# Order of VectorE's work in the adapter layer: experts chosen ahead of the turning of the next tile

## The chip, the cores and the metric

One Trainium2 chip, one of its cores. The time is the device time of one execution in microseconds (us); smaller is better.

## What is computed

64 sequences of 64 channels by 512 features go through two layers: a conditioned spline FFN, then an adapted linear layer (LoRA adapter chosen per sequence) whose output goes through a mixture of eight experts, two per token. The change is in the stage that computes the adapted layer and the routing of the second layer:

```python
H = jnp.einsum('btd,od->bto', x, W)
xa = jnp.einsum('btd,brd->btr', x, A[adapter_idx])
delta = jnp.einsum('btr,bor->bto', xa, Bm[adapter_idx]) * scalings[adapter_idx][:, None, None]
z = (H + delta).reshape(-1, 512)
top_w, sel = jax.lax.top_k(z @ gate_w.T, 2)
tw = jnp.zeros((n, 8)).at[arange(n)[:, None], sel].add(softmax(top_w))
out = einsum('end,ne->nd', down(silu(gate(z)) * up(z)), tw)
x = x + out
```

## The kernel before

The program has four stages: preparing the weights (about the first 60 us), the first FFN, the adapted layer (`adapted_layer`, about 500 to 660 us of the profiled execution), and the experts.

`adapted_layer` goes over 4096 tokens in 8 tiles of 512 (t = 0 to 7), each cut into four sub-tiles of 128 tokens (s = 0 to 3). Tiles 0, 1, 6 and 7 are written out, 2 to 5 are a loop with two tiles per pass. Each engine has a queue of its own, in the order in which the code is written, and all orders meet at semaphores. No scheduler moves anything.

Per tile t:

- TensorE (PE) multiplies x1 by the adapters' A for the whole tile (12 matmuls, L1439 to L1441, bank XA). Then come eight products of 15 matmuls (L1428), `product(t, b, s, half, chunks)`: the output row of 520 columns (512 outputs and 8 logits) is cut into two halves, the right half (half 1, which has the logits) of s = 0 to 3 first, then the left half (half 0) of s = 0 to 3. The first two right halves run their first 12 matmuls while VectorE and ScalarE scale and split `xa`, and then their last three. A product may start when its PSUM bank has been copied out: s = 0 and 2 share a bank in each half, as do s = 1 and 3. Last come the two small matmuls of `ranks(t)` (L1413, L1414), which count for each token the rows that its experts have before it. They wait for `both_ready`. In tile 6 (`is_late`) PE leaves after two left halves, and the rest of it and its ranks stand in tile 7.
- ScalarE (ACT) rounds `xa` (L1489), rounds the next tile's x1 in four pieces (`high`, L1475, waits for `x1_loaded`), copies each product out of PSUM (`copy`, L1484), rounds two pieces of the early experts' weights (L1505, waits for `early_loaded`), and takes the exponential of the logits' gap (`shares`, L1479). Its order in tiles 2 to 5: xa, high 0 and 1, copy of right halves 0 and 1, early pieces, high 2, right half 2, high 3, right half 3, the left halves, with the exponential after the third of them.
- VectorE (DVE) scales xa (L1617), makes its remainder (L1621), and for each s makes the remainder of the next tile's x1 (`low`, L1542) and turns that x1 into token order (`turn`, L1548), with the early weights' remainders (L1632) at s = 1. Then it chooses the two experts (`choose`, L1563 to L1583, a chain of small instructions that ends with `both_ready`), and makes the shares and row numbers (`enter`, L1596 to L1609). `choose` waits for the copies of the right halves 2 and 3.
- SyncE (SP) issues DMAs. `next_x1(t + 2)` loads x1 of the tile after the next (L403, two DMAs). There is one x1 buffer, so it waits until tile t + 1 has been remaindered and turned (`x1t_low`, `tok_turned`). Behind it stand `store_out(t + 1)` (L1364, four DMAs of the turned x1) and `load_early(t + 1)` (L363, two DMAs of early weights).
- GpSimd (POOL) waits for the row numbers and then scatters the tile's rows with eight indirect DMAs (L1403), each pair behind a small instruction (L1401).

Of the kernel before, what the change touches and what calls it, by code (L numbers as in the profile page):

```python
# [29 lines left out]
LSUB = LTILE // P  # L30
# [1241 lines left out]
def adapted_layer(nc, alloc, sem, psum, ident, small, idle, lower, ones, tok_ids, out_tiles, x1, x1_loaded, load_x1,  # L1272
# [5 lines left out]
    with ExitStack() as scope:  # L1278
# [52 lines left out]
        def is_late(t):  # L1331

            return isinstance(t, int) and t == LNT - 2

        def is_last(t):
            return isinstance(t, int) and t == LNT - 1

        def xa_of(t):
            return (xa_high[1], xa_low[1]) if is_last(t) else (xa_high[0], xa_low[0])
# [17 lines left out]
        with nc.Block() as block:  # L1357
# [50 lines left out]
            @block.tensor  # L1408
            def _(pe):
                def ranks(t):  # L1410

                    pe.wait_ge(both_ready, t + 1)
                    nc.tensor.matmul(psum[RANKS][:, 0:LSUB * NE], lower[:, :], both[:, :, :].rearrange("p s e -> p (s e)"), start=True, stop=False)  # L1413
                    nc.tensor.matmul(psum[RANKS][:, 0:LSUB * NE], ones[:, :], chosen[:, 0:LSUB, :].rearrange("p s e -> p (s e)"),  # L1414
                                     start=False, stop=True).then_inc(filled[RANKS], 1)

                def product(t, b, s, half, chunks):

                    hi, lo = x1t_hi[b], x1t_lo[b]
                    xa_hi, xa_lo = xa_of(t)  # L1420
                    bank, rows = Z[s % 2][half], slice(s * P, (s + 1) * P)
                    if 0 in chunks:
                        pe.wait_ge(drained[bank], use(t, s) + 1)
                    for k in chunks:
                        x_high, x_low = (hi[:, k, rows], lo[:, k, rows]) if k < DK else (xa_hi[:, rows], xa_lo[:, rows])
                        for i, (x, w) in enumerate(((x_high, w_hi), (x_high, w_lo), (x_low, w_hi))):
                            last = k == DK and i == 2
                            ins = nc.tensor.matmul(psum[bank][:, 0:HALFW], x, w[:, k, half * HALFW:(half + 1) * HALFW],  # L1428
                                                   start=(k == 0 and i == 0), stop=last)
                    if DK in chunks:  # L1430
                        ins.then_inc(filled[bank], 1)

                def body(t, n, b, has_next, first):

                    pe.wait_ge(x1t_low, LSUB * (t + 1))
                    hi, lo = x1t_hi[b], x1t_lo[b]
                    pe.wait_ge(drained[XA], t + 1)
                    for k in range(DK):
                        nc.tensor.matmul(psum[XA][:, :], a_hi[:, k, :], hi[:, k, :], start=(k == 0), stop=False)  # L1439
                        nc.tensor.matmul(psum[XA][:, :], a_hi[:, k, :], lo[:, k, :], start=False, stop=False)  # L1440
                        ins = nc.tensor.matmul(psum[XA][:, :], a_lo[:, k, :], hi[:, k, :], start=False, stop=(k == DK - 1))  # L1441
                    ins.then_inc(filled[XA], 1)
                    if is_last(t):
                        ranks(t - 1)

                    for s in range(2):
                        product(t, b, s, 1, range(DK))

                    pe.wait_ge(xa_done, t + 1)
                    for s in range(2):  # L1450
                        product(t, b, s, 1, [DK])
                    for s in range(2, LSUB):
                        product(t, b, s, 1, range(DK + 1))
                    if is_late(t):
                        for s in range(EARLIER):
                            product(t, b, s, 0, range(DK + 1))
                        return
                    if is_last(t):
                        for s in range(EARLIER, LSUB):
                            product(t - 1, 1 - b, s, 0, range(DK + 1))  # L1460
                        ranks(t)
                        nc.tensor.matmul(psum[XA][:, 0:NE], ones[:, :], chosen[:, LSUB, :], start=True, stop=True).then_inc(counted, 1)
                    for s in range(LSUB):
                        product(t, b, s, 0, range(DK + 1))
                    if not is_last(t):
                        ranks(t)

                steps(pe, body)

            @block.scalar  # L1470
            def _(act):
                def high(t, b, s):
                    if s == 0:
                        act.wait_ge(x1_loaded, 32 * (t + 1))
                    nc.scalar.activation(x1t_hi[b][:, :, s * P:(s + 1) * P], x1[:, :, s * P:(s + 1) * P], ACT.Copy).then_inc(x1t_high, 1)  # L1475

                def shares(t):
                    act.wait_ge(gap_ready, t + 1)
                    nc.scalar.activation(expo[:, :], gap[:, :], ACT.Exp).then_inc(expo_ready, 1)  # L1479

                def copy(t, b, s, half):
                    bank = Z[s % 2][half]
                    act.wait_ge(filled[bank], use(t, s) + 1)
                    nc.scalar.activation(z_out[b][:, s, half * HALFW:(half + 1) * HALFW], psum[bank][:, 0:HALFW], ACT.Copy).then_inc(drained[bank], 1)  # L1484

                def body(t, n, b, has_next, first):

                    act.wait_ge(drained[XA], t + 2)
                    nc.scalar.activation(xa_of(t)[0][:, :], xa[:, :], ACT.Copy).then_inc(xa_split, 1)  # L1489
                    if first and b == 0:  # L1490
                        copy(t, b, 0, 1)
                        copy(t, b, 1, 1)
                    if has_next:
                        for s in range(2):
                            high(t + 1, 1 - b, s)
                    if not first:

                        act.wait_ge(rows_stored[b], 16 * 2 * LSUB * n)
                    if not (first and b == 0):
                        copy(t, b, 0, 1)  # L1500
                        copy(t, b, 1, 1)
                    act.wait_ge(early_loaded, 16 * EARLY * (t + 1))
                    for e in range(EARLY):
                        to, _, raw = early_piece(t, b, e)
                        nc.scalar.activation(to, raw, ACT.Copy).then_inc(early_high, 1)  # L1505
                    for s in range(2, LSUB):
                        if has_next:
                            high(t + 1, 1 - b, s)
                        copy(t, b, s, 1)
                    if is_late(t):  # L1510
                        for s in range(EARLIER):
                            copy(t, b, s, 0)
                        shares(t)
                        return
                    if is_last(t):
                        for s in range(EARLIER, LSUB):
                            copy(t - 1, 1 - b, s, 0)
                        shares(t)
                    for s in range(LSUB):
                        copy(t, b, s, 0)  # L1520
                        if s == LSUB - 2 and not is_last(t):
                            shares(t)

                for s in range(LSUB):
                    high(0, 0, s)
                steps(act, body)

                nc.scalar.activation(idle[:, 63:64], small[:, 0:1], ACT.Silu)
                act.wait_ge(ctl_ready, 1)
                fetch_quads(act, 0, 0, (2, 3), rows_there)  # L1530

            @block.vector
            def _(dve):
# [78 lines left out]
                def body(t, n, b, has_next, first):  # L1612
# [11 lines left out]
                    for s in range(LSUB):  # L1624
                        if has_next:
                            low(t + 1, 1 - b, s)
                            turn(t + 1, s)
                        if s == 1:
                            for e in range(EARLY):
                                hi, lo, raw = early_piece(t, b, e)  # L1630
                                dve.wait_ge(early_high, EARLY * t + e + 1)
                                ins = nc.vector.tensor_tensor(lo, raw, hi.bitcast(F32), ALU.subtract)  # L1632
                                ins.then_inc(*((early_low, 1) if has_next else (weights_loaded, LOADS)))
                    choose(t, b)
                    if not is_late(t):
                        enter(t, n, b, first)

# [376 lines left out]
```

## Time and profile before

| | us |
|---|---|
| median of 3 runs | 1139.07 |
| lowest, highest run | 1135.13, 4557.15 |
| the profiled execution's own time | 1139.03 |
| span of its profile | 1137.3 |
| PE busy in the span | 1047.3 (92%) |
| DVE, ACT, POOL busy | 693.9, 473.1, 655.5 |

The span is the time between the first and the last instruction of the profile; the 1.7 us around it are launch and end. Tiles of the adapted layer follow each other every 18.4 to 18.8 us in the middle.

### The profile page before, as it was taken

Reading aid. Unit: us, or ns where it says so; the run is one execution under the profiler, and the core shown is the slowest. Engines: PE = TensorE matmul, PEld = TensorE weight load, DVE = VectorE, ACT = ScalarE, POOL = GpSimd, SP = SyncE. Lnnn points to the kernel's source line nnn. Section 1 sums busy time; section 2 is a strip of 40 time slices with the busy share of each in tenths; the row PEclk is TensorE's granted clock in tenths of the full one; section 3 lists DMA queues with packets and bytes.
Section 4 is the critical chain, followed back from the end, with each engine's and each line's share of the span. In section 5 each row is a group of like instructions: output and inputs, shape, how many; then the busy total and the mean of one; then the engine's idle time right before and its main releaser. Section 6 shows DMA issues by size and latency. Waiting matters only on the chain. (4 is left out here: it accounts for less than half of the span.)

```text
span 1137.3 us, 35583 instructions
## 1 busy us (share of the span) xinstructions
PE 1047.3 (92%) x12060; PEld 969.1 (85%) x12061; DVE 693.9 (61%) x1478; ACT 473.1 (42%) x964; POOL 655.5 (58%) x889
## 2 busy tenths in 40 slices
PE   1679999999999999879999949999999999999995
PEld 1669999999999999779999938999999999999994
DVE  8945666666776666447676735555555555555553
ACT  4245776777767767524333212222222222222221
POOL 6568999999999999603455533333333333333333
PEclk9868999999999999969999969999999999999998
DMA  6052555455555553446878658586767676745453
GB/s 263 1 165 102 199 177 183 164 197 200 184 174 200 175 183 128 184 131 199 275 236 278 193 177 234 97 230 145 182 146 174 144 179 142 186 83 83 84 87 61
DMA packets 126612, 188.32 MB, mean 166 GB/s; under 512 B 26040, under 2 KB 89656, under 8 KB 123104
## 3 DMA queue, kind: packets, MB, share of 16 engines
q1 hardware_dynamic: 58560, 130.96, 34.4%
q0 software_dynamic: 16432, 36.78, 16.4%
q10 hardware_dynamic: 51584, 20.12, 7.1%
q8 instruction: 21, 0.34, 0.1%
q14 instruction: 15, 0.12, 0.0%
HBM read 108.37 MB, written 81.83 MB: 167 GB/s over the span
## 5 line engine op out<-in xcount | busy, mean ns | idle before, releaser
L1760 POOL TENSOR_TENSOR idle<-small 128x1 f32<-128x1 f32 x212 | 71.1, 338 | 269.9 <-DMA out<-result,scatter_at 194.7
L1803 PE MATMUL banks<-slots,zt_hi 128*128 x568 | 189.3, 333 | 16.1 <-DVE zt_lo L1914 16.1
L1805 PE MATMUL banks<-slots,zt_lo 128*128 x568 | 183.9, 324 | 0.0
L1804 PE MATMUL banks<-slots,zt_hi 128*128 x568 | 183.9, 324 | 0.0
L985 POOL TENSOR_TENSOR in_lo<-inner,in_hi 128x512 fp32r<-128x512 f32 x128 | 164.4, 1291 | 31.9 <-ACT in_hi L1133 31.6
L1222 DVE TENSOR_TENSOR inner<-silu,banks 128x512 f32<-128x512 f32 x128 | 87.9, 687 | 113.7 <-ACT silu L1128 109.5
L1871 ACT ACTIVATE ht_hi<-banks 128x384 fp32r<-128x384 f32 x71 | 35.0, 492 | 253.5 <-PE banks L1813 246.0
L1776 POOL DMA_INDIRECT out<-result,scatter_at x71 | 111.6, 1572 | 28.1 <-issue 26.2
L1803 PEld LDWEIGHTS banks<-slots,zt_hi 128*128 128x128 f32 x568 | 107.5, 189 | 16.3 <-issue 16.3
L979 POOL TENSOR_TENSOR f_lo<-f_sum,f_hi 128x256 fp32r<-128x256 f32 x128 | 110.7, 884 | 3.1 <-ACT f_hi L1124 3.1
L1128 ACT ACTIVATE silu<-banks 128x512 f32<-128x512 f32 x128 | 76.3, 596 | 77.1 <-PE banks L1054 75.9
L1804 PEld LDWEIGHTS banks<-slots,zt_hi 128*128 128x128 f32 x568 | 107.6, 189 | 0.0
L1805 PEld LDWEIGHTS banks<-slots,zt_lo 128*128 128x128 f32 x568 | 107.4, 189 | 0.0
L1133 ACT ACTIVATE in_hi<-inner 128x512 fp32r<-128x512 f32 x128 | 80.5, 629 | 42.3 <-DVE inner L1222 31.0
L1944 DVE TENSOR_TENSOR result<-banks,share 128x512 f32<-128x512 f32 x71 | 49.1, 692 | 76.9 <-DMA out<-result,scatter_at 55.6
L1054 PE MATMUL banks<-f_hi,gu_hi 64*128 64x256 f32 x512 | 87.1, 335 | 7.3 <-DVE inner L1222 4.4
L1881 ACT ACTIVATE zt_hi<-banks 128x512 fp32r<-128x512 f32 x72 | 43.1, 598 | 104.7 <-DVE banks L384 91.3
L1212 DVE TENSOR_REDUCE f_sum<-banks 128x256 f32<-128x512 f32 x128 | 82.1, 683 | 5.8 <-PE banks L1040 5.4
L1823 PE MATMUL banks<-slots,ht_hi 128*128 x213 | 84.2, 395 | 1.3 <-DVE ht_lo L1918 1.3
L1825 PE MATMUL banks<-slots,ht_lo 128*128 x213 | 84.4, 396 | 0.0
L1070 PE MATMUL banks<-in_hi,down_hi 32*128 32x256 f32 x1024 | 83.7, 316 | 0.6 <-POOL in_lo L985 0.6
L1824 PE MATMUL banks<-slots,ht_hi 128*128 x213 | 84.0, 394 | 0.0
(255 smaller groups left out, 3136.7 us busy)
## 6 DMA issues: line engine op xcount, KB each, us to landing
late_dram<-split_part SPq DMA_DIRECT2D x32, 816.0 KB, 5.2
slots<-late_dram SPq DMA_DIRECT2D x24, 1088.0 KB, 5.6
x<-rows_dram ACTq DMA_DIRECT2D x278, 64.0 KB, 3.2
raw_part<-in_late_w SPq DMA_DIRECT2D x16, 816.0 KB
x_t<-in_x_t SPq DMA_DIRECT2D x16, 512.0 KB
x_both<-in_x_tok SPq DMA_DIRECT2D x16, 512.0 KB
x_both<-in_x_res SPq DMA_DIRECT2D x16, 512.0 KB, 3.4
x1t_dram<-x_both SPq DMA_DIRECT2D x16, 512.0 KB, 6.3
```

Of the source, the lines that this page charges most:

```text
L979: nc.gpsimd.tensor_tensor(f_lo[:, g, :], f_sum[g % F_SUMS][:, :], f_hi[:, g, :].bitcast(F32), ALU.subtract).then_inc(f_done, 1)
L985: nc.gpsimd.tensor_tensor(in_lo[:, cs, :], inner[u % 2][:, :, :], in_hi[:, cs, :].bitcast(F32), ALU.subtract).then_inc(in_done, 1)
L1054: ins = nc.tensor.matmul(gu_bank[:, h, m * TILE:(m + 1) * TILE], w[rows, m, cols], f[rows, u, :], start=(i == 0), stop=(i == 2))
L1070: ins = nc.tensor.matmul(out_bank[r][:, cols], w[rows, c, :], x[rows, c, :], start=(c == 0 and i == 0), stop=(c == IC - 1 and i in (2, 4)) ...
L1222: nc.vector.tensor_tensor(inner[u % 2][:, :, :], silu[u % 2][:, :, :], gu_bank[:, :, TILE:2 * TILE], ALU.mult).then_inc(gu_drained, 1)
L1776: nc.gpsimd.indirect_dma_start(out, bass.IndirectOffsetOnAxis(ap=scatter_at[b][:, 0:1], axis=0), result[b][:, :], None, compute_op=ALU.add ...
L1803: nc.tensor.matmul(psum[bank][:, 0:FD], zt_hi[b][:, k, :], w_high, start=(k == 0), stop=False)
L1804: nc.tensor.matmul(psum[bank][:, 0:FD], zt_hi[b][:, k, :], w_low, start=False, stop=False)
L1805: ins = nc.tensor.matmul(psum[bank][:, 0:FD], zt_lo[b][:, k, :], w_high, start=False, stop=(k == DK - 1))
L1823: nc.tensor.matmul(psum[OUT[b]][:, :], ht_hi[:, f, :], w_high, start=(f == 0), stop=False)
L1824: nc.tensor.matmul(psum[OUT[b]][:, :], ht_hi[:, f, :], w_low, start=False, stop=False)
L1825: ins = nc.tensor.matmul(psum[OUT[b]][:, :], ht_lo[:, f, :], w_high, start=False, stop=(f == FC - 1))
```

## The change

Three calls move and nothing is added or left out. VectorE makes the four turns of the next tile's x1 between `choose` and `enter` instead of one behind each `low`. ScalarE takes the exponential after the second copy of a left half instead of the third. TensorE makes `ranks(t)` ahead of the last left half instead of behind it.

```diff
@@ PE
                     for s in range(LSUB):
                         product(t, b, s, 0, range(DK + 1))
-                    if not is_last(t):
-                        ranks(t)
+                        if s == LSUB - 2 and not is_last(t):
+                            ranks(t)
@@ ACT
                     for s in range(LSUB):
                         copy(t, b, s, 0)
-                        if s == LSUB - 2 and not is_last(t):
+                        if s == 1 and not is_last(t):
                             shares(t)
@@ DVE
                     for s in range(LSUB):
                         if has_next:
                             low(t + 1, 1 - b, s)
-                            turn(t + 1, s)
                         if s == 1:
...
                     choose(t, b)
+                    if has_next:
+                        for s in range(LSUB):
+                            turn(t + 1, s)
                     if not is_late(t):
                         enter(t, n, b, first)
```

VectorE in tile 0, between the remainder of xa and the choice (L1542 is `low`, L1548 `turn`, L1632 and its new number L1631 the early weights), the difference:

```order
-L1542 TENSOR_TENSOR x1t_lo<-x,x1t_hi 128x4x128
-L1548 STREAM_TRANSPOSE x_tok<-x 128x4x4x32
-L1542 TENSOR_TENSOR x1t_lo<-x,x1t_hi 128x4x128
-L1548 STREAM_TRANSPOSE x_tok<-x 128x4x4x32
-L1632 TENSOR_TENSOR slots<-slots 128x544 x2
-L1542 TENSOR_TENSOR x1t_lo<-x,x1t_hi 128x4x128
-L1548 STREAM_TRANSPOSE x_tok<-x 128x4x4x32
-L1542 TENSOR_TENSOR x1t_lo<-x,x1t_hi 128x4x128
-L1548 STREAM_TRANSPOSE x_tok<-x 128x4x4x32
+L1542 TENSOR_TENSOR x1t_lo<-x,x1t_hi 128x4x128 x2
+L1631 TENSOR_TENSOR slots<-slots 128x544 x2
+L1542 TENSOR_TENSOR x1t_lo<-x,x1t_hi 128x4x128 x2
```

The four transposes have gone from here.

VectorE in the same tile, from the end of `choose` (L1583) to the start of `enter` (L1596), the difference:

```order
 L1581 TENSOR_TENSOR staging<-staging 128x32
 L1583 TENSOR_TENSOR chosen<-chosen,staging 128x8 x4
+L1548 STREAM_TRANSPOSE x_tok<-x 128x4x4x32 x4
 L1596 TENSOR_SCALAR total<-expo 128x4
 L1597 RECIPROCAL staging<-total 128x4
```

They stand here now, behind the 16 steps of the choice; the next x1 load, the stores of the turned x1 and the early weights' load wait for the last of them on SP's queue.

TensorE at the end of tile 0 before (L1413 and L1414 are the ranks, L1439 and L1440 belong to the next tile):

```order
L1428 MATMUL banks<-w_lo,xa_hi 128x260
L1428 MATMUL banks<-w_hi,xa_lo 128x260
L1413 MATMUL banks<-staging,lower 128x32
L1414 MATMUL banks<-chosen,ones 128x32
L1439 MATMUL banks<-x1t_hi,a_hi 128x512
L1440 MATMUL banks<-x1t_lo,a_hi 128x512
```

And at the end of the third left half now:

```order
L1428 MATMUL banks<-w_lo,xa_hi 128x260
L1428 MATMUL banks<-w_hi,xa_lo 128x260
L1413 MATMUL banks<-staging,lower 128x32
L1414 MATMUL banks<-chosen,ones 128x32
L1428 MATMUL banks<-w_hi,x1t_hi 128x260
L1428 MATMUL banks<-w_lo,x1t_hi 128x260
```

The ranks stand 15 matmuls sooner, ahead of the product of the last sub-tile.

## Rows read from the trace of the kernel before

**Rows 1.** Windows: length, busy of PE, PEld, DVE, ACT, POOL; clock, DMA share, GB/s

```profile
502.00:508.20 6.20, 5.46 (x13) 4.30 (x14) 3.09 (x6) 0.00 (x0) 0.00 (x0) 0.50 0.24 69
...
564.90:583.70 18.80, 17.88 (x138) 17.16 (x137) 12.31 (x42) 6.89 (x16) 10.14 (x12) 1.00 0.80 263
```

**Rows 2.** Timeline of PE: start, length, instruction, idle before it and what ended it

```profile
502.74 0.80 PE L1439 MATMUL banks<-x1t_hi,a_hi 128*128 128x512 f32 x1 [4.26 <-DVE x1t_lo L1542]
...
524.17 0.41 PE L1413 MATMUL banks<-staging,lower 128*128 128x32 f32 x2 [0.97 <-DVEq L1584]
...
580.15 0.31 PE L1413 MATMUL banks<-staging,lower 128*128 128x32 f32 x2
...
580.52 0.48 PE L1439 MATMUL banks<-x1t_hi,a_hi 128*128 128x512 f32 x1
...
588.05 0.39 PE L1428 MATMUL banks<-w_hi,x1t_hi 128*128 128x260 f32 x1 [0.92 <-ACT staging L1484]
```

**Rows 3.** Timeline of DVE: tile 0's turns, then tiles 1, 3, 6 and 7

```profile
502.60 2.49 DVE L1548 STREAM_TRANSPOSE x_tok<-x 128x512 f32<-128x512 f32 x4
...
519.87 0.70 DVE L1548 STREAM_TRANSPOSE x_tok<-x 128x512 f32<-128x512 f32 x1
...
537.82 0.14 DVE L1563 TENSOR_REDUCE top<-x_both 128x4 f32<-128x32 f32 x1
...
573.29 0.70 DVE L1548 STREAM_TRANSPOSE x_tok<-x 128x512 f32<-128x512 f32 x1
574.05 0.19 DVE L1563 TENSOR_REDUCE top<-x_both 128x4 f32<-128x32 f32 x1
...
576.89 0.77 DVE L1583 TENSOR_TENSOR chosen<-chosen,staging 128x8 f32<-128x8 f32 x4
...
583.69 0.69 DVE L1617 TENSOR_TENSOR xa<-banks,adapter_scale 128x512 f32<-128x512 f32 x1 [1.93 <-issue]
...
629.71 0.14 DVE L1563 TENSOR_REDUCE top<-staging 128x4 f32<-128x32 f32 x1
...
643.61 0.19 DVE L1563 TENSOR_REDUCE top<-x_both 128x4 f32<-128x32 f32 x1 [0.76 <-issue]
```

**Rows 4.** Timeline of ACT in tiles 0, 1, 3 to 4, and 7

```profile
515.27 0.62 ACT L1475 ACTIVATE x1t_hi<-x 128x512 fp32r<-128x512 f32 x1
...
533.42 1.21 ACT L1505 ACTIVATE slots<-slots 128x544 fp32r<-128x544 f32 x2 [1.05 <-DMA slots<-in_early_w]
...
535.32 0.62 ACT L1475 ACTIVATE x1t_hi<-x 128x512 fp32r<-128x512 f32 x1
...
573.56 0.39 ACT L1484 ACTIVATE x_both<-banks 128x260 f32<-128x260 f32 x1 [1.30 <-PE banks L1428]
...
584.95 1.14 ACT L1475 ACTIVATE x1t_hi<-x 128x512 fp32r<-128x512 f32 x2
...
588.16 1.21 ACT L1505 ACTIVATE slots<-slots 128x544 f32 x2
...
640.73 1.21 ACT L1505 ACTIVATE slots<-slots 128x544 fp32r<-128x544 f32 x2 [1.25 <-DMA slots<-in_early_w]
```

**Rows 5.** SP's DMA issues behind the turns of tile 3

```profile
574.24 1.32 SPq L403 DMA_DIRECT2D x<-x1t_dram  x2
575.75 4.74 SPq L1364 DMA_DIRECT2D out<-x_tok  x4
580.73 2.22 SPq L363 DMA_DIRECT2D slots<-in_early_w  x2
```

**Rows 6.** DMA view, 500 to 660 us (the landing times: 574 to 576 us)

```profile
q0 software_dynamic: 4749, 15.84, 25.7%
...
rows_dram<-staging,row_i POOLq DMA_INDIRECT x32
rows_dram<-x_both,row_i POOLq DMA_INDIRECT x30
...
DMA to landing us min/median/max: 4.8/5.7/6.6
```

## The prediction

> **What bounds the kernel now.** I read the page first: PE is busy for 92% of the span, and the adapted layer is no exception. The windows show a middle tile as 18.80 us with PE busy for 17.88 [rows 1]. The timeline of PE has the rest: one wait of 0.92 us per middle tile, for the copy of the first right half (an idle stretch that the change does not aim at), and two places where the ranks wait for the choice of experts, 0.97 us in tile 0 and a like one in the last tile. In tiles 1 to 5 the ranks wait for nothing, as at 580.15 [rows 2]. So PE's queue has about 1 us to gain, in tile 0, since the last tile's order stays as it is.
>
> Then I read what the three other queues do, because the turns release DMAs. Call C the start of a tile's choice on DVE and T the end of the next tile's turns. Before, T comes just ahead of C: the last turn of tile 3 ends at 573.99, the choice starts at 574.05 [rows 3]. It could hardly start sooner, for the copy of the last right half, on which it waits, ends at 573.95 [rows 4]. At T, SP issues two loads of x1, four stores and two loads of early weights, one behind the other: from 574.24 to 582.95, thus until T + 9.0 [rows 5]. The reader is to see how much room ACT leaves for these: x1 is taken at 584.95, 11.0 us after T, the early weights at 588.16, 14.2 us after T. In tile 1 ACT did wait for the early weights (taken at 533.42, with T at 520.57: 12.85 us), and in tile 7 as well [rows 3, 4].
>
> **The change part by part.** *The choice ahead of the turns, DVE.* Nothing is added: four turns of 2.49 us leave one place and enter another [rows 3]. In tile 0 C is bound by DVE's own work. The last piece of x1 from ACT is there at 515.89 [rows 4], and behind it stand some 1.4 us of remainders, so C goes from 520.5 to 517.3, 3.2 us sooner; the ranks then don't wait, 0.97 us saved on PE. In tile 1 C could gain 0.9, in tiles 3 to 5 nothing, as the copy at 573.95 ends last.
>
> *What the turns release.* T becomes C plus the choice, 576.89 + 0.77 - 574.05 = 3.6, plus 2.5 for the turns: C + 6.1 in place of C - 0.1. For tile 3 that is 580.15, 6.2 us later. The next x1 landed 575.0 + 6.6 = 581.6 before, T + 7.6 [rows 6]; so it lands at C + 13.7 or later, while ACT wants it at C + 10.9: 2.8 us late, and with two roundings (1.14) and a copy (0.4) ahead of it PE's third right half starts near C + 15.3. PE is there at C + 12.3 (choice 3.6, ranks 0.4, last product 1.8, the A matmuls 583.69 - 580.52 less 0.4 = 2.8, two right halves without xa 3.6). So its 0.92 us wait becomes 3.0.
>
> *The early weights close a loop.* ACT takes them at T + 12.85 in tile 1, when it is waiting. Between them and the copy of the last right half stand 535.32 + 0.62 - 533.42 = 2.5 us of ACT's own work and that copy, 0.4: C of this tile is 2.9 us behind the landing at the soonest [rows 4]. Thus C -> T (6.1) -> early weights -> C of the next tile (2.9). All are in the queues' order, and the next round starts from the late C.
>
> *How long the DMAs take.* Lower bound: 13.0 from T, the row of tile 1 and a little more, as the middle tiles carry more traffic. Upper bound: POOL's eight scatters per tile began 8 us after T before and will begin about 2 us after it, since the row numbers come from `enter` right behind the turns. So about 4.5 more of them go beside the loads. The software queue took 25.7% of 160 us for 62 scatters, 0.66 us each [rows 6]; 4.5 of them are 3.0 us of all 16 engines, or 2.6 at the share above 1 that loaded stretches show. Upper bound 15.6, middle 14.3, and I take the middle, as it is not seen in the trace who gives way.
>
> The Trainium skill (DMA: Bandwidth & Descriptors, section "Queues, rings and completion order") says that each DMA engine goes round robin between the queue rows it has work for, a packet at a time. By that, SP's loads do give way to the scatters, and the value would be nearer 15.6; by the row of tile 1 alone it would be 13.0. The trace of before does not show eight scatters beside the loads.
>
> *The loop's period* is 6.1 + 14.3 + 2.9 = 23.3 us, against (629.71 - 537.82) / 5 = 18.4 from C of tile 1 to C of tile 6 [rows 3]. PE's work fits: 17.9 plus the waits of 3.0 for x1 (more if x1 is slowed too) and 1.4 for the choice. The latter is new: PE's third left half can start only after ACT's copy of the first at C + 0.4, ends at C + 2.3, and then the ranks, now one product sooner, wait until C + 3.7. The ranks' new place thus costs nothing by itself, since that wait lies within the loop's period; nor does the exponential, which waits for a result inside the choice, as the third copy is not filled much before then.
>
> *The sum.* C of tile 1: 517.3 + 6.1 = 523.4, early weights 13.4 later (half of a small contention), 2.9 more: 539.7 against 537.8, +1.9. Five rounds to tile 6: 5 x 23.3 = 116.5 against 91.9, +24.6. From tile 6 to 7 SP has no x1 to load: 640.73 - 629.8 = 10.9 from T; ACT has no x1 to round either, 1.9 from landing to C. Together 6.1 + 10.9 + 1.9 = 18.9 against 643.61 - 629.71 = 13.9, +5.0. In that tile PE then stands for some 6 us. After a wait of 4.26 us it ran at a granted clock of 0.50, 1.2 GHz [rows 1, 2]; one product at that clock costs 1.8 us more before the last scatters can start, of which I count half, +0.9. From there the tail and the experts are as before. Sum +32.4 on the profiled execution's 1139.0: 1171. The median of the runs shown is 1139.07, so nothing has to be shifted.
>
> With 13.0 from T the sum is 1.3 + 18.1 + 5.0 = +24.4, 1163; with 15.6 it is 2.5 + 31.1 + 5.0 + 1.8 = +40.4, 1179. Two percent of the time, about what a measurement of this kernel can tell from no change, is 22.8 us.
>
> **The rivals.** *The loads stay hidden* (ends on the other side). For the period to stay 18.8, the early weights must land within 18.8 - 6.1 - 2.9 = 9.8 us of T. Then all that is left is the 0.97 us of tile 0: 1138. For it: in the middle tile shown ACT finds the weights there, with 14.2 - 13.0 = 1.2 us to spare. Against: SP has not even issued the second load before T + 9.0.
>
> *It is late once and does not feed back.* If a late C did not make the next tile late, as PE's own waits would give the queues time to catch up, the cost would be one round and the last tile: 1.9 + 4.9 + 5.0, 1151. For it: the DMA engines are at 0.80 share and get lighter with a longer tile. Against: the loop holds latencies and one queue's issue time more than bandwidth.
>
> *The clock falls in every tile.* PE's wait for x1 gets near the 4.26 us after which half the clock was granted. Two right halves at 1.2 GHz cost 3.6 us, which fits in the time until the early weights; two more products at that clock add 3.6 us to each of five tiles: 1171 + 18 = 1189. For it: contention lengthens just this wait. Against: a lower clock fills the gap that causes it.
>
> The Trainium skill (TensorE: Matmul & The Clock Gate, section "Part 1: The HAM clock gate (the "warmup" mystery)") has the array at 1.2 GHz when it was idle and at 2.4 GHz when it is kept busy; the row at 502.00 with its 0.50 agrees, and by that page alone this rival would have more than the chance that I give it.
>
> **How the numbers follow.** The loop as worked out: 0.80, of it 0.08 below the 2% (some latency shorter than in tile 1). The clock in every tile: 0.08. Late once: 0.06. Hidden: 0.06, a third of it faster by over 2%, as the trace of before might understate what waits. So slower 0.72 + 0.08 = 0.80, same 0.08 + 0.06 + 0.04 = 0.18, faster 0.02. The range reaches from 1155, below the loop's lower bound and short of the late-once case, to 1188, just below the clock's.
>
> **What would show it.** In the changed profile ACT's early weights (L1505) wait for their DMA in tiles 1 to 7, 4 to 6 us in the middle; L1475 waits 3 to 4 us for x1 from tile 2 on; PE waits about 3 us for the copy ahead of the third right half and 1.4 us for the choice ahead of the ranks; C follows C at 22 to 24.5 us; the scatters start 2 us after the turns. In tile 0 the ranks wait for nothing. It is wrong if ACT finds the early weights there and tiles stay at 18.8 us, or if the period grows while the waits stand at PE's half clock. The term I trust least is the 14.3.

## The result, and the profile after

The changed kernel takes 1199.04 us (median of 4 runs, 1197.69 to 1201.91) against 1139.34 us for the kernel before on the same chip. The ratio is 1.055, with a 95% interval of 1.0509 to 1.059; it leaves out one run of the kernel before, of 4557 us, which the median holds. Slower was forecast, by 32 us; it is 60 us slower, and the time lies above the range. The profiled execution of the changed kernel has a span of 1196.0 us, 58.7 more than before.

The head of the page of the changed kernel, with engine, busy time, share, instructions:

```profile
span 1196.0 us, 35583 instructions
PE 1068.8 (89%) x12060; PEld 988.3 (83%) x12061; DVE 693.0 (58%) x1478; ACT 472.4 (39%) x964; POOL 649.0 (54%) x889
```

The instructions are the same in number. PE is busy for 21.5 us more with the same matmuls, which fits the lower clock shown below (the first matmul behind the long wait takes 0.58 us; in [rows 2] it was 0.39); the other engines are busy for about as long as they were, POOL for 6.5 us less. The rest of the 58.7 us is waiting.

The timeline of DVE in the changed kernel, with the first instruction of each tile's choice (C) for tiles 1 to 5, and the turns behind those of tiles 1 and 3:

```profile
544.65 0.18 DVE L1563 TENSOR_REDUCE top<-x_both 128x4 f32<-128x32 f32 x1
...
548.40 2.49 DVE L1548 STREAM_TRANSPOSE x_tok<-x 128x512 f32<-128x512 f32 x4
...
572.12 0.18 DVE L1563 TENSOR_REDUCE top<-staging 128x4 f32<-128x32 f32 x1
...
598.95 0.18 DVE L1563 TENSOR_REDUCE top<-x_both 128x4 f32<-128x32 f32 x1
...
602.79 2.49 DVE L1548 STREAM_TRANSPOSE x_tok<-x 128x512 f32<-128x512 f32 x4 [0.24 <-DVE chosen L1583]
...
626.91 0.18 DVE L1563 TENSOR_REDUCE top<-staging 128x4 f32<-128x32 f32 x1
...
654.38 0.18 DVE L1563 TENSOR_REDUCE top<-x_both 128x4 f32<-128x32 f32 x1
```

C follows C at 27.5, 26.8, 28.0 and 27.5 us; before it was 18.4 on average [rows 3]. In tile 0 C is at 516.68 in place of 520.49, so the choice did come sooner where DVE alone set it. From tile 1 on it is late, and later each time.

What ScalarE waits for shows why. Its timeline in tiles 3 and 4 of the changed kernel, the rows that answer to those of [rows 4]:

```profile
584.99 1.16 ACT L1475 ACTIVATE x1t_hi<-x 128x512 fp32r<-128x512 f32 x2 [0.50 <-DMA x<-x1t_dram]
...
595.63 1.20 ACT L1505 ACTIVATE slots<-slots 128x544 f32 x2 [8.62 <-DMA slots<-in_early_w]
...
611.79 1.16 ACT L1475 ACTIVATE x1t_hi<-x 128x512 fp32r<-128x512 f32 x2 [0.23 <-DMA x<-x1t_dram]
...
623.59 1.20 ACT L1505 ACTIVATE slots<-slots 128x544 f32 x2 [9.52 <-DMA slots<-in_early_w]
...
626.01 0.93 ACT L1484 ACTIVATE staging<-banks 128x260 f32<-128x260 f32 x3
```

Both waits of the prediction are there, but not in their sizes: x1 costs 0.2 to 0.7 us in tiles 2 to 5 (1.7 and 2.7 in tiles 1 and 6), the early weights 8.6 to 9.5 in tiles 2 to 6 (10.3 in tile 1, 7.1 in tile 7). Once they are there, ScalarE waits for nobody: the row at 626.01 is the copy of the fourth right half and of two left halves in one go, so their products had long been made, and C follows at 626.91. And SP's issues behind the turns that end at 605.28:

```profile
605.50 1.32 SPq L403 DMA_DIRECT2D x<-x1t_dram  x2
607.01 4.15 SPq L1364 DMA_DIRECT2D out<-x_tok  x4
611.40 5.19 SPq L363 DMA_DIRECT2D slots<-in_early_w  x2
```

Against [rows 5], the x1 load and the stores are issued at the old pace, and the issue of the early weights takes 5.19 us in place of 2.22. ScalarE takes them at 623.59, 18.3 us behind the last turn; before it was 12.9 to 14.2 in tiles 1 to 6.

TensorE ahead of the third left half and of the ranks, in tile 4 of the changed kernel:

```profile
626.71 0.58 PE L1428 MATMUL banks<-w_hi,x1t_hi 128*128 128x260 f32 x1 [5.50 <-ACT staging L1484]
...
630.62 0.64 PE L1413 MATMUL banks<-staging,lower 128*128 128x32 f32 x2 [0.29 <-DVEq L1584]
```

(The product at 626.71 is the third left half, which waits for the copy of the first out of their common bank; the third and fourth right half are long made.) One such wait of 4.6 to 6.2 us has come in each of tiles 1 to 5; the one ahead of the ranks is only 0.3 us there. Behind tile 6 TensorE stands for 5.1 us, and 5.7 us ahead of the ranks of tile 7. The windows from C to C, with the columns of [rows 1]:

```profile
core 0: us, PE busy (x) PEld busy (x) DVE busy (x) ACT busy (x) POOL busy (x), PEclk, DMA share, GB/s
572.12:598.95 26.83, 21.81 (x137) 20.62 (x138) 12.17 (x42) 6.85 (x17) 9.26 (x12) 0.82 0.57 179
598.95:626.91 27.96, 22.05 (x137) 20.79 (x138) 12.15 (x42) 6.86 (x17) 9.58 (x12) 0.81 0.54 171
```

And two windows of 3 us in tile 3, ahead of the long wait and behind it:

```profile
590.00:593.00 3.00, 3.00 (x27) 3.00 (x26) 0.00 (x0) 0.00 (x0) 1.43 (x2) 1.00 0.99 351
...
599.00:602.00 3.00, 3.00 (x15) 3.00 (x15) 2.55 (x17) 0.21 (x1) 0.00 (x0) 0.50 0.00 0
```

The granted clock is 0.81 on average: 2.4 GHz (1.00) up to the long wait, and 1.2 GHz (0.50) behind it, while TensorE makes the third and fourth left half. And the DMA engines, 0.80 busy before, are down to 0.54 over the tile: they are loaded while ScalarE waits (0.99), and idle while VectorE chooses and turns (0.00).

### The profile page after: what moved, and what is told of

Same layout as the page of the kernel before. It is cut to its first block and busy times, and to the rows that moved or that the text cites. A ratio compares the mean times of both kernels' runs of the same rounds, so it can differ in the third digit from the quotient of the medians.

```text
span 1196.0 us, 35583 instructions
## 1 busy us (share of the span) xinstructions
PE 1068.8 (89%) x12060; PEld 988.3 (83%) x12061; DVE 693.0 (58%) x1478; ACT 472.4 (39%) x964; POOL 649.0 (54%) x889
## 5 line engine op out<-in xcount | busy, mean ns | idle before, releaser
L1762 POOL TENSOR_TENSOR idle<-small 128x1 f32<-128x1 f32 x212 | 70.7, 336 | 273.0 <-DMA out<-result,scatter_at 189.9
L1805 PE MATMUL banks<-slots,zt_hi 128*128 x568 | 189.3, 333 | 14.3 <-DVE zt_lo L1916 14.3
L1428 PE MATMUL banks<-w_hi,x1t_hi 128*128 128x260 f32 x256 | 80.7, 315 | 30.4 <-ACT x_both L1484 17.2
L1401 POOL TENSOR_TENSOR idle<-small 128x1 f32<-128x1 f32 x32 | 7.8, 245 | 154.3 <-DVE row_i L1609 146.4
```

The source lines that it names most:

```text
L1805: nc.tensor.matmul(psum[bank][:, 0:FD], zt_hi[b][:, k, :], w_high, start=(k == 0), stop=False)
```

## The experiments

Each kernel was compared with the kernel before on the same chip. C, T (end of the turns) and "landing" (ScalarE takes the early weights) are as in the prediction.

The stages ahead of the adapted layer vary between the profiled executions (TensorE begins on the layer at 496.1 to 506.4 us), so these executions are compared by the layer alone as well: from TensorE's first matmul in it (502.74 in the kernel before, [rows 2]) to the ranks of the last tile.

| kernel | us |
|---|---|
| before | 144.6 |
| changed | 201.3 |
| only VectorE's move | 205.7 |
| only the ranks' and the exponential's moves | 147.6 |
| early weights' load first | 145.0 |
| scatters held back | 172.0 |
| two of four turns | 198.9 |
| wait filled with matmuls | 205.5 |
| left half first | 141.1 |
| left half and early weights' load first | 141.1 |
| the same, turns behind the choice in tile 0 | 147.7 |

### Only VectorE's move

```diff
-                        if s == LSUB - 2 and not is_last(t):
-                            ranks(t)
+                    if not is_last(t):
+                        ranks(t)
...
-                        if s == 1 and not is_last(t):
+                        if s == LSUB - 2 and not is_last(t):
                             shares(t)
```

Here and below, the edit is against the changed kernel unless said otherwise.

> Only VectorE's move is made; ranks and exponential stay in their old places. Theory L (a loop: late turns hold up SP's loads, these hold up ScalarE and the next choice): the period of a tile is set off PE, so this is as slow as the change whole, 1195 to 1203 us, tiles every 27.4 us. Rival P (the ranks' new place, a wait of TensorE ahead of a product, is part of the loss): well below, under 1185 us.

1203.73 us, ratio 1.055 (1.0495 to 1.0606). That is 0.7 us above the upper end of what was expected. From tile 1 to tile 6 the choices stand 27.1 to 29.3 us apart. VectorE's move alone brings the whole loss, and rival P is out. Whether the other two soften it by a few us stays open: the layer takes 4 us more here than in the changed kernel, and the interval is some 6 us to either side. One thing differs: in tiles 2 to 6 ScalarE waits 2.4 to 4.0 us for x1, besides 8.6 to 10.9 for the early weights.

### Only the ranks' and the exponential's moves

```diff
                             low(t + 1, 1 - b, s)
+                            turn(t + 1, s)
...
                     choose(t, b)
-                    if has_next:
-                        for s in range(LSUB):
-                            turn(t + 1, s)
```

> Only the ranks' and the exponential's moves are made; the turns stay behind each remainder. Theory L: no loop, tiles every 18.8 us, 1138 to 1143 us; the ranks wait some 2.7 us in tile 0 instead of 1.0. Rival P: clearly slower than before, over 1150 us.

1140.71 us, ratio 1.0037 (1.0008 to 1.0066). The time is as expected: no loop, and a small loss of 3.6 us, of which the layer shows 3.0. The two moves without the first put the ranks of tile 0 into a longer wait, of 4.35 us in place of 0.97; 2.7 was expected.

```profile
523.83 0.64 PE L1413 MATMUL banks<-staging,lower 128*128 128x32 f32 x2 [4.35 <-DVEq L1584]
```

### The early weights' load ahead of the x1 load

```diff
                     if has_next:
+                        if not (first and b == 0):
+                            sp.wait_ge(early_low, EARLY * t)
+                        load_early(sp, t + 1, 1 - b)
                         if not (isinstance(t, int) and t == LNT - 2):
                             next_x1(t + 2)
                         store_out(t + 1)
-                        if not (first and b == 0):
-                            sp.wait_ge(early_low, EARLY * t)
-                        load_early(sp, t + 1, 1 - b)
```

The load no longer stands behind the wait for the turns, on which it does not depend.

> The change whole, but SyncE issues the early weights' load ahead of the x1 load that waits for the turns. Theory L: ScalarE no longer waits for the early weights; what is left of the loop is C to turns 6.3, x1 landing 6.5, two roundings and a copy 1.6, two right halves 3.6, copy 0.5 = 18.5 us, so 1138 to 1146 us. Rival W (TensorE's clock, halved in each tile, sets the period): the clock still falls and the time stays over 1170 us.

1137.67 us, ratio 0.9996 (0.9969 to 1.0024): all 60 us are back, by a change of SP's order alone. The timeline of ScalarE in tile 3 of this kernel:

```profile
567.07 1.15 ACT L1475 ACTIVATE x1t_hi<-x 128x512 fp32r<-128x512 f32 x2 [1.29 <-DMA x<-x1t_dram]
568.66 1.20 ACT L1505 ACTIVATE slots<-slots 128x544 f32 x2
```

The early weights cost no wait any more. x1 costs 1.3 to 2.0 us per tile, and the choices stand 18.3 to 19.2 us apart, where the working gave 18.5. The time is 0.3 us below the range that was expected. So the turns' late place costs the 60 us through the early weights' load, which SP has queued behind them; the x1 load, which still waits for the turns, costs nothing that the runs can tell.

### The scatters held back

```diff
                     pool.wait_ge(entries_ready, t + 1)
+                    if has_next and not is_late(t):
+                        pool.wait_ge(early_loaded, 16 * EARLY * (t + 2))
```

> The change whole, but GpSimd begins tile t's scatters only when the early weights of t + 1 have landed (tiles 0 to 5). Theory L with contention by the scatters: from the last turn to the early weights 13 us instead of 17.8, period 22.6, so 1163 to 1175 us. Rival S (SyncE's issues and the loads alone take 17.8 us, with or without scatters): 1195 us or more.

1165.31 us, ratio 1.0261 (1.0214 to 1.0309). The turns that end at 588.39 and what follows, in SP's issues and on ScalarE (the added lines shift the numbers by two):

```profile
588.61 1.32 SPq L403 DMA_DIRECT2D x<-x1t_dram  x2
590.12 5.30 SPq L1364 DMA_DIRECT2D out<-x_tok  x4
595.67 2.37 SPq L363 DMA_DIRECT2D slots<-in_early_w  x2
```

```profile
601.08 1.21 ACT L1507 ACTIVATE slots<-slots 128x544 f32 x2 [3.58 <-DMA slots<-in_early_w]
```

Without scatters beside them the early weights land 12.7 us behind T, and SP's issue of them is back at 2.4 us. Rival S is out. This splits the loss roughly in two: the loop with the old latency costs some 28 us, and the scatters that now run beside the loads the other half. (The held-back scatters reach up to the next turns here and slow x1 a little, which is taken 7.1 to 7.4 us behind T in tiles 3 to 6, so the 28 us are rather too much for the latency alone.)

### Two of the four turns behind the choice

```diff
                             low(t + 1, 1 - b, s)
+                            if s < 2:
+                                turn(t + 1, s)
...
                     if has_next:
-                        for s in range(LSUB):
+                        for s in range(2, LSUB):
                             turn(t + 1, s)
```

> The change with only the turns of sub-tiles 2 and 3 behind the choice; 0 and 1 stay behind their remainders. Theory L: every us by which the last turn comes sooner after the choice's start leaves the period: 1.25 us in six rounds, 7.5 us less, 1189 to 1194 us. Rival W (TensorE's half clock sets the period): no change from 1199 us.

1192.92 us, ratio 1.0474 (1.0393 to 1.0556). The median is inside what the loop theory expects; the interval is too wide to tell 7.5 us from nothing on its own. The choices stand 25.4, 25.3, 27.2, 28.1, 27.4 and 27.3 us apart: the gain is seen in the first rounds and is given back in the later ones, where the landing takes 18.8 to 19.7 us from T in place of 16.9 to 17.2. The expectation was an equal gain of 1.25 us in each of six rounds, so its median is right in part by luck. Half a move costs nearly as much as the whole, which fits a queue that waits for the last turn and not for the number of them.

### TensorE's wait filled with matmuls

```diff
                         product(t, b, s, 1, [DK])
+                    if not (first and b == 0) and not is_last(t):
+                        for i in range(30):
+                            nc.tensor.matmul(psum[1][:, 0:HALFW], hi[:, i % DK, 0:P], w_hi[:, i % DK, 0:HALFW], start=True, stop=True)
                     for s in range(2, LSUB):
                         product(t, b, s, 1, range(DK + 1))
```

> The change whole, and TensorE runs 30 more matmuls of 128x260 (3.6 us at full clock, their result is not used) in tiles 1 to 6 ahead of the third right half, where it waits 5 us. Theory L (the loop runs over VectorE, SyncE, the DMAs and ScalarE, TensorE has room in it): the clock stays at 1.00 in the middle tiles and the time stays at 1195 to 1203 us, the matmuls cost nothing. Rival W (the half clock after each wait is a part of the loss): with the clock up the time falls under 1190 us.

1199.8 us, ratio 1.0547 (1.0495 to 1.0599). The windows of this kernel:

```profile
548.00:576.00 28.00, 24.19 (x171) 23.15 (x172) 11.96 (x42) 6.64 (x16) 9.45 (x12) 0.92 0.53 172
...
576.00:603.00 27.00, 23.08 (x159) 21.90 (x158) 11.20 (x40) 6.56 (x16) 9.24 (x12) 0.88 0.56 178
```

From C to C the clock was 0.84, 0.94, 0.87, 0.92 and 0.84, where it was 0.81 to 0.82 in most tiles (not 1.00, as was expected: a wait of 2 to 5 us is left). The choices stand 28.0, 28.1, 28.6, 28.1 and 27.9 us apart, no less where the clock is at 0.94 than where it is at 0.84, and the runs show no cost of 30 matmuls more per tile (the layer of the profiled execution is 4 us longer than the changed kernel's, the median of the runs 0.8). The expectation had the place of the wait wrong by four products: it stands ahead of the third left half, as the profile above shows, and not ahead of the third right half. The matmuls delay the products between, and shorten the wait all the same. So TensorE is off the path that sets the period, and its lower clock is a consequence of the loss. The clock was raised only in part, but with ScalarE's rows above, in which the products for the choice are made before the early weights land, rival W is out.

### The left half of sub-tile 0 ahead of the third right half

Against the kernel before (the same loops for tiles 6 and 7 start one sub-tile later to match):

```diff
+                    if not is_last(t):
+                        product(t, b, 0, 0, range(DK + 1))
                     for s in range(2, LSUB):
                         product(t, b, s, 1, range(DK + 1))
...
-                    for s in range(LSUB):
+                    for s in range(0 if is_last(t) else 1, LSUB):
                         product(t, b, s, 0, range(DK + 1))
...
                         if has_next:
                             high(t + 1, 1 - b, s)
+                        if s == 2 and not is_last(t):
+                            copy(t, b, 0, 0)
                         copy(t, b, s, 1)
```

> The kernel before, but TensorE makes the left half of sub-tile 0 between the right halves of 1 and 2 (all tiles but the last), and ScalarE copies it there. If the 0.9 us wait of TensorE in each middle tile is only the copy of the first right half's bank, it goes in tiles 1 to 6, and the ranks still wait for nothing: 1134 to 1136 us. Rival: the choice, now 1.8 us later, becomes what the ranks wait for, and the time stays at 1138 to 1141 us.

1135.19 us, ratio 0.9966 (0.9938 to 0.9994). TensorE's 0.92 us wait per middle tile [rows 2] is gone, and the ranks still wait only in tile 0 (1.8 us in place of 1.0) and tile 7. The tiles stand 17.75 us apart on average, in place of 18.4. ScalarE now waits 0.7 to 1.7 us for the early weights in each tile, but TensorE does not wait for ScalarE.

### The same with the early weights' load first

The edit of SP's order and that of the left half together, against the kernel before.

> The kernel before with the left half of sub-tile 0 ahead of the third right half, and SyncE issuing the early weights' load ahead of the x1 load. If ScalarE's waits for the early weights (0.7 to 1.7 us per tile when only the left half is moved) held anything up, this is 1 to 4 us faster than that version, 1132 to 1134 us; if TensorE alone sets the pace, the same 1135 us.

1130.51 us (12 runs), ratio 0.9947 (0.9923 to 0.9971). It is faster than the kernel before, and 1.5 us under the range that was expected. But the early weights' load has no share in this that the runs show: the intervals of this kernel and of the last one overlap, and the layer takes 141.1 us in both, 3.5 less than before. ScalarE's waits for the early weights are gone, and the layer is no shorter for it. The rest of the difference lies ahead of the layer, on which TensorE began at 496.1 us in this profiled execution, and at 503.6 and 502.7 in those of the last version and the kernel before; why is open. The window of a middle stretch:

```profile
560.00:578.00 18.00, 18.00 (x141) 17.48 (x140) 12.78 (x42) 7.22 (x18) 10.97 (x13) 1.00 0.78 256
```

TensorE is busy without a break, as it already was in the last version (88.76 of 88.76 us from the choice of tile 1 to that of tile 6). What is left of waits on it in the layer is 1.7 us in tile 0 and 0.6 in the last tile, both ahead of the ranks.

### And the turns behind the choice in tile 0 alone

To the last version:

```diff
                             low(t + 1, 1 - b, s)
-                            turn(t + 1, s)
+                            if not (first and b == 0):
+                                turn(t + 1, s)
...
                     choose(t, b)
+                    if first and b == 0:
+                        for s in range(LSUB):
+                            turn(t + 1, s)
```

> As the left-half and early-load version, with the turns behind the choice in tile 0 alone. The ranks' wait in tile 0 (1.8 us with the left half moved) goes: 1.8 us faster than without it, 1131 to 1133 us. If the later turns cost as much through the next x1 load as they save, no difference.

1140.57 us, ratio 1.0018 (0.9992 to 1.0044): neither of the two, but 10 us slower than the version without it, of which 6.6 are in the layer; the profiled execution also began on the layer 6.5 us later. The wait in tile 0 is gone, and tile 1 has a larger one. The timeline of VectorE and TensorE there (L1552 is the turn):

```profile
532.00 0.69 DVE L1546 TENSOR_TENSOR x1t_lo<-x,x1t_hi 128x512 fp32r<-128x512 f32 x1 [3.95 <-ACT x1t_hi L1477]
539.16 0.71 DVE L1552 STREAM_TRANSPOSE x_tok<-x 128x512 f32<-128x512 f32 x1 [6.47 <-DMA out<-x_tok]
```

```profile
548.33 0.64 PE L1413 MATMUL banks<-staging,lower 128*128 128x32 f32 x2 [6.25 <-DVEq L1588]
```

The first turn of tile 2 overwrites what the store of tile 1 reads, so it waits for that store, which was issued late because the turns of tile 1 were. In tile 1 the choice stands behind that turn, 26.9 us behind the one of tile 0 in place of 18.3, and the ranks wait 6.25 us for it. The changed kernel is spared this one, since its turns stand behind the choice in all tiles.

## Why the prediction was right or wrong

**Right: the mechanism.** What bounds the layer, the loop from the choice over the turns, SP's queue and the early weights' landing to ScalarE and the next choice, and the sign. With the turns moved, the order of SP's queue alone makes or undoes the loss (the early load first: 60 us back). The rival that the loads stay hidden, and the one that they are late only once, are wrong.

**Right: the smaller terms.** The choice and the turns took 6.2 to 6.3 us (6.1 was said), from the landing to C 3.2 to 3.3 (2.9; what ends last there is not the copy but VectorE's remainders of the early weights and of x1), from tile 6 to tile 7 18.8 us (18.9), the tail after the last ranks 1.7 us more (0.9). The landing from T in tile 6, where SP loads no x1 and the first scatter starts only 4.4 us behind T, was 10.6 us, and 10.9 before. C of tile 0 came 0.6 us sooner than said (516.7 for 517.3).

**Wrong: one term, "How long the DMAs take".** I took 14.3 us from T to the early weights (13.4 in tile 1), with 15.6 as the upper bound. The changed kernel shows 17.2 to 18.6, 17.9 on average. That is 5.2 us too little in tile 1 and 2.9 to 4.0 in each of tiles 2 to 6, 22.5 of the 26 us by which the sum fell short of the profiled execution's 1197.7; the 0.4 and 0.2 us per round of the smaller terms and the tail make up the rest. By tile: C of tile 1 was 6.8 us late (1.9 said), five rounds of 27.4 us in place of 23.3 added 45 (24.6 said).

Where the upper bound failed can be seen in its own working. I counted 0.58 us of DMA time for each further scatter. A scatter moves 128 rows of 520 numbers, 0.27 MB, so that is some 460 GB/s; no window of 2 us of the trace before moved more than 371. The share of engine time by queue was no price for added work. With the rate of the stretch the bound would have been 17.3, the low end of what came. The windows from T to the landing, of the kernel before (tile 3) and of the changed one (tile 4):

```profile
573.99:588.16 14.17, 13.25 (x100) 12.53 (x100) 8.51 (x36) 3.87 (x10) 6.20 (x8) 1.00 0.87 282
```

```profile
605.28:623.59 18.31, 15.82 (x111) 14.85 (x110) 4.09 (x15) 2.92 (x6) 9.58 (x12) 0.94 0.83 260
```

18.31 us at 260 GB/s are 4.8 MB, which is all that a tile moves: x1 and its store 1.05 MB each, the early weights 0.56, eight scatters 2.13. The early weights landed at the end of it, together with the last scatters, at 623.5. 4.5 scatters at 282 GB/s are 4.3 us and not 2.6, and 13.0 + 4.3 = 17.3 (an estimate). The kernel with the scatters held back measured the same term without them, 11.7 to 13.1 us in tiles 1 to 6: that the scatters take the difference is shown.

The Trainium skill's rule of a round robin between the queue rows (DMA: Bandwidth & Descriptors, section "Queues, rings and completion order") pointed to the upper end, and the runs agree: the loads did give way, with 17.2 to 18.6 us beside the scatters and 11.7 to 13.1 without. That rule says who gives way, not by how much; the rate had to come from the windows.

**Wrong: where TensorE waits.** I put 3.0 us ahead of the third right half, for x1, and 1.4 ahead of the ranks. The waits for x1 were under a microsecond in tiles 2 to 5, for two reasons. ScalarE asked for x1 later than I had it, in tile 4 at C + 12.6 (C of tile 3) in place of C + 10.9, since TensorE had made two left halves at 1.2 GHz, and the A matmuls behind them came late. And x1 landed some 6.5 us behind T and not 7.6. A likely cause is that the last two scatters of a tile, issued at 572.81 and 574.55 in the kernel before, no longer stand beside it; this was not tried by itself, and where only VectorE's move was made x1 was taken 6.1 to 7.2 us behind T without such scatters. The long wait came ahead of the third left half, for ScalarE, which was held at the early weights. The copy that frees that bank stands behind the early weights in ScalarE's order, so the bank was released late.

**The clock rival** had the lower clock right and its price wrong. The clock did fall behind the long wait of each tile from 1 on, and the time is nearer to that rival's 1189 than to the forecast, but by luck: with the wait filled and the clock raised in part the time stays, so the lower clock costs nothing that the runs show while the loop is the longer chain.

**The gain in tile 0** (0.97 us) was there: the ranks wait for nothing in it.

## What to carry to other kernels

When work is moved that releases DMAs, list what stands behind that wait on the issuing queue, and how much time each consumer had to spare; here 1.2 us of spare time met a shift of 6.2. If the consumer in turn holds up the moved work, the shift is paid in every round. Price traffic that comes together by the bytes and the rate of a loaded window (here 0.94 us for a scatter), not by a queue's share of engine time (0.58). And put a load that does not depend on the wait ahead of the ones that do: with that, all turns behind the choice cost nothing that the runs could tell. It is no licence to move them at will, since the turns moved in tile 0 alone made the next tile's turns wait for a store, and the layer 6.6 us longer.

## What the runs showed that was not expected

- One product moved in TensorE's queue took 3.5 us out of the layer. With the early load moved as well, TensorE was busy for 18.00 of 18.00 us and the median was 0.5% under the kernel before (1130.51 us), but the layer was no shorter for it.
- A short issue is not a property of the instruction: two DMAs of early weights took SP 2.0 to 2.6 us to issue in tiles 0 to 5 of the kernel before, 1.8 to 3.2 there with the scatters held back, and 3.6 to 5.2 in the changed kernel, with the scatters beside them. The scatters need not be all of it: in tile 6 of the kernel before, with the last one started 3.4 us earlier, it was 3.7.
- TensorE's 0.92 us wait in each middle tile also went in the kernel that moves only the ranks and the exponential, though neither touches the bank in question. Why ScalarE's copy of the first right half starts 0.8 us after the last matmul for it in the kernel before, and at once there, was not tried and stays open. In tiles 2 to 5 that copy also has to wait for the scatters of the tile two before it, which share its buffer; the trace does not show whether they ended last.
